# Octonion FFN and top-2 mixture of experts on one core: ten experts of the ranking, instead of eight, keep separate places for the tokens of the two halves

## What is computed

```python
x = x + L0_ffn(L0_cond(x))
y = L1_cond(x)                      # a small mixed kernel per batch
logits = y @ gate_w.T               # 32 experts
w, idx = top_k(logits, 2); w = softmax(w)
# out[token] = sum over its two experts of w * (y[token] @ W_e.T + b_e)
x = x + out
```

## Time and profile before

| what | value |
|---|---|
| three runs, median | 314.0 us (312.17 to 316.85) |
| the profiled execution, its own time | 315.92 us |
| its span from first to last instruction | 314.0 us |
| PE busy with matmuls | 281.8 us (90%) |
| DVE, ACT, POOL busy | 122.7, 81.7, 73.7 us |
| mean granted TensorE clock | 0.968 |
| moved by DMA | 58.11 MB, mean 185 GB/s |

### The profile page before, as it was taken

The page is one execution under the profiler, slowest core; times in us unless marked ns, Lnnn a source line. Parts: engine busy times, 40 slices in busy tenths (PEclk is TensorE's granted clock), DMA queues, the critical chain, the costliest instruction groups (busy, mean ns, idle before and its releaser), DMA issues.

```text
span 314.0 us, 4114 instructions
## 1 busy us (share of the span) xinstructions
PE 281.8 (90%) x1442; PEld 186.4 (59%) x1442; DVE 122.7 (39%) x354; ACT 81.7 (26%) x150; POOL 73.7 (23%) x74
## 2 busy tenths in 40 slices
PE   3998989999999999999999999988999999999000
PEld 2698977777887777878887774323334445333000
DVE  0357441655630333456540455324524111110085
ACT  3345245555421113323321112110101111111000
POOL 0022331000000000003604222437354555422100
PEclk9999999999999999999999999999999999999755
DMA  7990000000000000009119953939999999951398
GB/s 267 366 314 0 2 0 0 4 0 0 0 2 33 33 35 33 0 3 355 48 33 371 394 228 81 387 90 335 400 419 420 421 417 415 357 223 64 112 392 349
DMA packets 17413, 58.11 MB, mean 185 GB/s; under 512 B 4288, under 2 KB 5952, under 8 KB 13168
## 3 DMA queue, kind: packets, MB, share of 16 engines
q1 hardware_dynamic: 11760, 46.95, 38.6%
q0 software_dynamic: 4192, 8.43, 7.6%
q10 hardware_dynamic: 1440, 2.46, 2.1%
HBM read 51.23 MB, written 10.85 MB: 198 GB/s over the span
## 4 chain that ended last, share of the span: by engine, by line
PE 80%; DMA 9%; issue 3%; DVE 3%; SPq 1%; ACT 1%; POOL 1%; POOLq 0%; ACTq 0%
PE bank L1048 26%; PE bank L1146 21%; PE bank L1182 13%; PE bank L970 7%; DMA parts<-r_tab 4%; PE bank L1119 3%; PE bank L1056 2%; PE bank L980 2%; PE bank L1077 2%; DMA slots<-kept,sid 1%; DMA xp<-in_xp 1%; PE bank L1002 1%; DMA yg<-y_tab,recs 1%; PE bank L1063 1%; SPq L455 1%
## 5 line engine op out<-in xcount | busy, mean ns | idle before, releaser
L1146 PE MATMUL bank<-wbuf,xT 128*64 128x512 f32 (+2 forms) x352 | 84.3, 598 | 0.0
L1146 PEld LDWEIGHTS bank<-wbuf,xT 128*64 128x64 f32 (+2 forms) x352 | 26.8, 139 | 39.0 <-issue 38.6
L469 POOL DMA_INDIRECT slots<-kept,sid x16 | 15.9, 994 | 122.9 <-DVE sid L809 119.9
L1182 PE MATMUL bank<-md,hhi 128*128 128x512 f32 x88 | 38.4, 437 | 0.0
L842 DVE COPY xT<-bank 128x512 f32<-128x512 f32 x23 | 15.9, 691 | 54.4 <-PE bank L1119 54.4
L1048 PE MATMUL bank<-y0hi,mg 128*128 128x512 f32 x88 | 36.0, 410 | 1.1 <-issue 1.1
L647 ACT ACTIVATE res<-bank,recs 128x512 f32<-128x512 f32 x23 | 15.8, 687 | 79.8 <-PE bank L1146 79.8
L1182 PE MATMUL bank<-md,hlo 128*128 128x512 f32 x88 | 34.5, 392 | 0.0
L1048 PE MATMUL bank<-y0lo,mg 128*128 128x512 f32 x88 | 34.4, 391 | 0.0
L1048 PE MATMUL bank<-y0hi,mu 128*128 128x512 f32 x88 | 34.2, 389 | 0.0
L1048 PE MATMUL bank<-y0lo,mu 128*128 128x512 f32 x88 | 34.2, 389 | 0.0
(11 more groups left out here) (163 smaller groups left out, 299.0 us busy)
## 6 DMA issues: line engine op xcount, KB each, us to landing
wbuf<-in_w SPq DMA_DIRECT2D x32, 1024.0 KB, 11.7
parts<-r_tab SPq DMA_DIRECT2D x8, 512.0 KB, 6.6
acc<-in_x SPq DMA_DIRECT2D x1, 2048.0 KB, 15.0
y_tab<-yv SPq DMA_DIRECT2D x8, 256.0 KB, 2.8
out<-acc ACTq DMA_DIRECT2D x8, 256.0 KB, 6.1
base<-in_base SPq DMA_DIRECT2D x3, 352.0 KB, 5.5
xp<-in_xp SPq DMA_DIRECT2D x1, 1040.0 KB, 10.2
slots<-in_pads SPq DMA_DIRECT2D x1, 576.0 KB, 16.0
```

Of the source, the lines that this page charges most:

```text
L469: pool.indirect_dma_start(out=slots, out_offset=bass.IndirectOffsetOnAxis(ap=sid[:, j, k:k + 1], axis=0), in_=rec[:, j, k], in_offset=None ...
L1146: v = mm(RS[t % 2][p0:p0 + w], xT[t % 2][:, c, p0:p0 + w], wbuf[buffer(r)][:, c], start=(c == 0), stop=(c == DC - 1))
L1182: v = mm(DN[j % 2][:], h[:, c, P * t:P * (t + 1)], md[:, c], start=(c == 0 and part == 0), stop=(c == HC - 1 and part == 1))
```

## The change

SPLIT goes from 8 to 10, so that FIRST, the number of early tiles, is 5. FULL goes from 8 to 6. Early tiles 0 to 4 have ranks (i, i+5), tiles 5 to 9 their second positions, tile 10 is the one with the positions 128 to 159, tiles 11 to 16 are full (ranks 10 to 15), and tiles 17 to 22 are as before. There are still 23. MIDDLE is 10, so one more matrix is loaded in the middle and one less after the last `down`. The buffers yg and res change places in memory; yg[4] lies where hhi and md were, so its gather waits for the last `down` (d_mm). GpSimd issues it behind the records of the seventh tile of tokens. PE takes transposes and product of the fifth early tile ahead of bias(0). All steps written with FIRST move by one tile with it.

```diff
-EARLY, MIDDLE, SOON = 3, 9, 12
+EARLY, MIDDLE, SOON = 3, 10, 12
+YE, RE = 4, 3
...
-SPLIT, NQ, FULL, PAIRS, QUADS = 8, 4, 8, 4, 2
+SPLIT, NQ, FULL, PAIRS, QUADS = 10, 4, 6, 4, 2
...
-def pairs(rank, pos):
-    return [[(PAIR * q, PAIR, rank + i + PAIRS * q, pos) for q in range(2)] for i in range(PAIRS)]
+def pairs(rank, pos, n):
+    return [[(PAIR * q, PAIR, rank + i + n * q, pos) for q in range(2)] for i in range(n)]
...
-TILES = (pairs(0, 0) + pairs(0, PAIR)
+TILES = (pairs(0, 0, FIRST) + pairs(0, PAIR, FIRST)
...
-         + pairs(NA, 0)
+         + pairs(NA, 0, PAIRS)
...
-SECOND = (4, 5, 6, 7, 0, 1, 2, 3) + tuple(range(8, NA))
+SECOND = tuple(range(NQ, SPLIT)) + tuple(range(NQ)) + tuple(range(SPLIT, NA))
...
-        yg = [ex.put(f"yg{i}", [P, D], F32) for i in range(FIRST)]
+        yg = [ex.put(f"yg{i}", [P, D], F32) for i in range(YE)]
...
-        res = [ex.put(f"res{i}", [P, D], F32) for i in range(U - 1)]
+        res = [ex.put(f"res{i}", [P, D], F32) for i in range(RE)]
...
-        yg += [ex.put(f"yg{i}", [P, D], F32) for i in range(FIRST, U)]
-        res += [ex.put(f"res{U - 1}", [P, D], F32)]
+        yg += [ex.put(f"yg{i}", [P, D], F32) for i in range(YE, U)]
+        res += [ex.put(f"res{i}", [P, D], F32) for i in range(RE, U)]
...
-            for t in range(FIRST):
+            for t in range(YE):
                 gather_tile(t)
-            for j in range(TPH, NT):
+            for j in range(TPH, NT - 1):
                 keep_record(j)
+            pool.wait_ge(d_mm, NT)
+            for t in range(YE, FIRST):
+                gather_tile(t)
+            keep_record(NT - 1)
             for t in range(2):
                 scatter(t, t, t)
-            pool.wait_ge(d_mm, NT)
...
-            product(3, 0, DC)
+            product(3, 0, 2)
+            transposes(4)
+            product(3, 2, DC)
+            product(4, 0, DC)
             pe.wait_ge(eb_in, 16)
             pe.wait_ge(combt_done, 2)
             bias(0)
```

## The result

Four runs of the kernel after have a median of 324.75 us (323.95 to 325.70), four of the kernel before 314.64 (312.17 to 316.85). The ratio is 1.035, with a 95% interval of 1.0277 to 1.0423: slower, by 8.7 to 13.3 us. The forecast was 324.5 in a range of 318.5 to 328.5. The profiled execution took 324.68 us, its span is 322.9.

A forecast was written before the change was run, and what follows sets the result against it. PE was taken to bound the kernel, with the expert matrix loads a second chain nearly as late. Terms 0.6 + 0 + 6.4 + 3.5 = +10.5 on 315.92 gave 326.4, or 324.5 us on the median 314.0; range 318.5 to 328.5.

The forecast's parts named there:

- Work on PE: Two full tiles go, one early and one second tile of two experts come: +0.6 us (0 to +1.0).
- The gap behind bias(0): PE's idle time before the next product stays, held by DVE's additions and copy instead of gathers: gain 0, at most 2.04.
- Early gather and memory places: Tile 4's gather is hidden in GpSimd's idle time and the memory layout costs nothing: 0, layout worst +1.
- The order of the loads: Rank 16's load waits for tile 9, going out at 239.6 instead of 217.3, with later loads behind it; rank 30 lands at 291.0.
- The stall: PE, ready for tile 21 at 284.6, waits for rank 30 until 291.0: +6.4 us (0 to 9.8).
- The clock: PE's clock falls during the wait, so tile 21 runs slow and tile 22 not: +3.5 us (0 to 7.05).
- The sum: Whole kernel: 0.6 + 0 + 6.4 + 3.5 = +10.5 us, giving 326.4, or 324.5 on the median.
- A: Rival: the stall is there, but the clock before the last tiles doesn't matter: +7.0, 321.0 us; chance 0.14.
- B: Rival: both last tiles run at 1.2 GHz behind the stall: +14.1, 328.1 us; chance 0.12.
- C: Rival: loads go no faster than 3.57 us each although fewer gathers run; stall 9.8, +13.9, 327.9 us; chance 0.10.
- D: Rival: the loads catch up, rank 30 lands by 284.6 without a stall; only 0.6 is left, 314.6 us; chance 0.10.
- E: Rival: no stall, and DVE's additions don't hold product 5 (-2.04): -1.4, 312.6 us; chance 0.04.

The follow-up runs named there:

- experiment 6: Experiment 1's kernel, with DVE copying xT of tiles 5 and 6 before adding the first four biases: 313.44 us, ratio 0.9966; run once more: 311.44 us, 0.9927.
- experiment 7: Kernel before with only DVE's order changed, xT of tiles 4 and 5 copied before the first four biases: 314.46 us, ratio 0.9983.
- experiment 1: Kernel after with only SECOND reordered to (5, 6, 7, 8, 4, 9, ...), so rank 16's load waits for tile 5, not tile 9: 318.63 us, ratio 1.006.
- experiment 2: Kernel before with only SECOND changed to (8, 4, 5, 6, 7, ...), so rank 16's load waits for tile 9: 328.46 us, ratio 1.0404.
- experiment 5: Kernel after with a bound of 0 for the gathers of tiles 14 to 22, which moves next to nothing and changes the computation: 315.76 us, ratio 1.0053.
- experiment 4: Kernel after with ten float32 matmuls of 512 columns on PE in front of tile 21: 326.35 us against 324.83 for the unchanged kernel after.

## Why the prediction was right, point by point

- **Work on PE, +0.6:** 0.45 by the trace.
- **The gap behind bias(0), 0:** right, and in the way it was put: the waits for gathers went, DVE's copy took their place at the same hour. From bias(0)'s end at 210.31 + 1.14 = 211.45 to product 5 at 214.65 are 3.20, for 3.24 predicted. Experiments 6 and 7 show both ends of it. The most it could give, 2.04, was near what experiment 6 got (from 3.20 to 1.36, that is 1.84).
- **Early gather and memory places, 0:** the gather was issued at 191.45, which is the 194.4 predicted less the earlier start, and no wait for it appears.
- **The order of the loads:** rank 16 was predicted at 239.6; less the 2.93 of the earlier start that is 236.7, where it was. Experiments 1 and 2 show that this order is the loss and is enough for it.
- **The stall, 6.4:** it measured 9.22 and 9.24, inside 0 to 9.8 and too small as a term. Rank 30 landed 53.9 us behind rank 16's issue, and not 4.8 + 35.7 + 10.9 = 51.4. What was mis-sized is the price of a gather. The prediction spread 15.2 us evenly over gathers and scatters, 0.56 each. Experiment 5 has 7.4 us for nine gathers, 0.82 each, where 0.56 gives 5.0: that is 2.4 of the 2.5 us by which rank 30 was late. The first load's 6.7 instead of 4.8 is part of it, as experiment 5 shows, and no term of its own. The scatters' 0.49 is what remains and was not measured by itself.
- **The clock, 3.5:** 2.2 to 2.4. It fell 3.5 us after PE's last transpose ended (281.5 to 285.0) and rose 4.5 us after tile 21's start, so only part of the two tiles ran slow. Experiment 4 shows the cause.
- **The sum:** the terms of the trace give 0.45 + 9.22 + 2.20 = 11.9 for the 10.5 forecast; the medians differ by 10.1, with 8.7 to 13.3 as the interval. The near agreement of 324.75 and 324.5 is partly luck: a stall too small by 2.8 is half set off by a clock term too large by 1.3, and the start, which differs by 2.9 us between executions, weighs more than the distance of the two numbers.
- **The rivals:** A falls by the slow last line. B falls, as the clock came back during the two tiles. C falls by experiment 5. D and E fall by the stall. The 358 GB/s of the Trainium skill ("DMA: Bandwidth & Descriptors", "Where 436 GB/s comes from") don't bound this kernel: loads alone land 2.55 us apart, 411 GB/s, and the window of the kernel after at 248 shows 412 GB/s of loads, gathers and scatters together.

## What to carry to other kernels

When a buffer is reused, go through the loads in the order in which an in-order queue issues them and note the release time of each; the first that is released late holds all the others, and a tuple of buffer numbers is as much part of the schedule as the tiles. Look at a queue's slack at its last user, not at its first: here DMA was mostly idle for 12 us without anyone waiting, and the bill came some 50 us later, with a slower clock on top. Where a pause on an engine has two releasers that end together, name both before taking one away; here either alone gave nothing.

## What the runs showed that was not expected

- The faster durations of TensorE begin at a different time in different executions: matmuls of one shape were still at 421 ns at 18.3 us in one and at 275 ns from about 14 us in another. It is some 2.9 us of the whole, as much as many a change is worth, so two single profiles can differ by it.
- A pause of 3.2 us with two groups of transposes in it can be enough for the clock to fall: with the same 2.18 us of idle time product 5 took 3.65 in the kernel after, where the granted clock stayed at 1.00, and 5.35 in experiment 4, where it fell at about 218.3. The diff between these two is 70 us later. In experiment 2 it fell behind two pauses of 1.06 and 1.01 us, and in experiment 7 two of 1.48 and 1.18 left product 4 at 3.65. What decides it stays open.
- In two executions (experiment 1 and the first of experiment 6) DVE started 1.7 and some 5 us late behind bias(0) with no engine that held it. The transfers in its stretch include blocks of the instruction queues at that time, but the executions without a late start have them as well; the cause stays open.
